# Graph attention kernel: first-tile scores straight from the parts of q and k, and softmax reciprocals turned by VectorE and spread by DMA

## The chip, the cores and the metric

The kernel runs on one core of one Trainium2 chip. The metric is device time in microseconds (us). Three runs of the kernel before took 1132.78, 1135.05 and 1135.31 us; the median is 1135.05 us.

## The reference

`x` is (8, 1024, 256), `adj` (1024, 1024) with zeros and ones, all fp32; there are 8 heads of 32 lanes.

```
h = relu(layernorm(x))
q, k, v = h @ Wq + bq, h @ Wk + bk, h @ Wv + bv          # split into 8 heads of 32
scores = einsum('bqhd,bkhd->bhqk', q, k) / sqrt(32) + (1 - adj) * -1e9
out = einsum('bhqk,bkhd->bqhd', softmax(scores), v)      # (b, n, 256)
x + out @ Wo + bo
```

## The kernel before

**Order of the work.** A batch is done in two phases of four heads (PHASES, g = 0 and 1). A phase has 32 rows; a row is one head h for one tile of 128 queries against all 1024 keys. Eight rows (two query tiles, four heads) are a unit; row r = 0 to 7 of it. Every engine walks over the same 8 x 2 x 32 = 512 rows in a function `slot`, and its order within a slot is written out by hand: tables with one entry per r (SCORES_AHEAD, MASK_AHEAD, EXP_AHEAD say how many rows ahead each step is; EXP_AT, HIGH_AT, COPY_AT, TAKE_AT say where in the slot it stands), STEPS (in which rows TensorE does the quarters, called pieces, of a projection) and ACT_COPIES (which rows' second copy ScalarE does; VectorE does the others). Engines are tied by semaphores alone.

**A row.** TensorE makes the scores (L703) from `q_stack` and `k_stack`. VectorE adds the mask and takes the row minimum (L550) into `rows`, a ring of four. ScalarE takes the exponential and the row's sum (L456). TensorE turns the row in eight 128x128 transposes (L717, `turn`) into the two banks `ps_turn`; ScalarE copies the first (L461), VectorE or ScalarE the second (L557, L466). `ps_scores` has two buffers, so that scores of row n wait for the mask of row n-2.

**The stacks.** q and k are each split into a high and a low float32r part (L471 on ScalarE, L562 on VectorE). Four parts of 32 lanes, stacked on the 128 partitions, make one full matmul give the exact product: (q_hi, q_lo, q_hi, q_lo) by (k_hi, k_hi, k_lo, k_lo). The parts go to the stacks by DMAs (L288, `stack_step`), 16 of 64 KB for 512 tokens. SP's queue issues them, at the start also GpSimd's and ScalarE's; SP also loads x, masks and residuals and stores the output.

**A unit's end.** In slot r = 7 VectorE takes the reciprocals of the sums (L585, `invert`), GpSimd spreads each over 32 columns (L425, `spread`), TensorE turns these in two transposes (L766, `turn_inv`), ScalarE copies them (L492, `copy_inv`). In slot 0 of the next unit TensorE multiplies the turned rows by v (64 matmuls, L780, `heads`) into `ps_heads`, and in slot 1 VectorE scales (L591, `norm_heads`). The output projection (L751) waits for that. `ps_heads` also takes the transposes of the next batch's normed x (L740), at HT_ROWS.

**The start.** TensorE projects q and k of all tokens (L724 in START_STEPS), then v (L733), then the row for the output bias (L812, added by L632), and then makes the scores of five rows, each after its stacks have landed, before the first `turn`. SP loads the masks of tiles 2 and 3 and stacks q's second half after the first four scores.

Of the kernel before, what the change touches and what calls it, by code (L numbers as in the profile page):

```python
# [10 lines left out]
P = 128  # L11
# [17 lines left out]


SCORES_AHEAD = (4, 5, 4, 4, 5, 4, 4, 5)
MASK_AHEAD = (4, 4, 4, 3, 3, 3, 3, 3)
EXP_AHEAD = (3, 2, 2, 2, 2, 2, 2, 1)
# [3 lines left out]
EXP_AT = (2, 2, 0, 0, 2, 2, 2, 0)  # L37
HIGH_AT = (0, 1, 1, 0, 0, 0, 1, 2)
COPY_AT = (0, 0, 0, 1, 1, 1, 1, 1)
TAKE_AT = (0, 1, 1, 0, 1, 0, 2, 2)  # L40
# [10 lines left out]
INV_ROW, NORM_ROW = 7, 1  # L51
# [3 lines left out]
def place(u, r):  # L55
# [28 lines left out]
STATS = (0, 1, 7, 7, 16, 23, 23, 23)  # L84

ACT_COPIES = (
    (2, 3, 4, 11, 13, 18, 21, 24, 27, 30),
    (0, 3, 6, 8, 10, 11, 13, 16, 19, 21, 24, 27, 29),
# [29 lines left out]
def gnn_kernel(nc, x, adj, Wq, bq, Wk, bk, Wv, bv, Wo, bo, out):  # L118
# [5 lines left out]
    with ExitStack() as ctx:  # L124
# [22 lines left out]
        start_parts = [nc.alloc_sbuf_tensor_at(f"start_{n}", [P, BANK], F32R, offset=turned_at + k * BANK * 4)  # L147
# [39 lines left out]
        ACT_HEADS = 2  # L187
# [107 lines left out]
        def _(sp):  # L295
# [76 lines left out]
        def _(pool):  # L372
# [44 lines left out]
            stack_step(pool, 0, 3, pool_stacked, range(ACT_HEADS, ACT_HEADS + 1))  # L417
# [17 lines left out]
            for b in range(BATCH):  # L435
                for g in range(PHASES):
                    for u in range(UNITS):
                        spread(b, g, u)
                        if (b, g, u) == (0, 0, 0):
                            late_masks(3, MASKS_LATE, TILES)  # L440
# [11 lines left out]
        def _(act):  # L452
# [52 lines left out]
            act.wait_ge(lo_done, START_QK.index(3) + 1)  # L505
            stack_step(act, 0, 3, start_stacked, range(ACT_HEADS))
            for n in range(EXP_AHEAD[-1]):
                exp(n)

            def slot(b, g, i, first, last):  # L510
                n, r = row(b, g, i), i % UNIT_ROWS
                pb, pg, kind, s = step_ended(b, g, i)
                if r == 0 and not (first and i == 0):
                    copy_inv(unit(b, g, i // UNIT_ROWS) - 1)
# [5 lines left out]
                if (g, i - 1) in HT_ROWS and not last:  # L520
                    copy_ht(b + 1, HT_ROWS[g, i - 1])
# [15 lines left out]
            copy_inv(BATCH * BATCH_UNITS - 1)  # L537

        @block.vector
        def _(dve):  # L540
# [39 lines left out]
            def invert(b, g, u, first):  # L580
                dve.wait_ge(exp_done, row(b, g, u * UNIT_ROWS) + UNIT_ROWS)
                if not (first and u == 0):

                    dve.wait_ge(inv_spread, unit(b, g, u))
                nc.vector.reciprocal(row_inv[:], row_sum[:, u % 2, :]).then_inc(inv_done, 1)  # L585

            def norm_heads(k, g, u):
                dve.wait_ge(inv_copied, k + 1)
                dve.wait_ge(heads_done, k + 1)
                dst = heads_t[0][:, u * UNIT_Q:(u + 1) * UNIT_Q] if g == 0 else heads_t[1][:, u % 2, :]  # L590
                nc.vector.tensor_tensor(dst, ps_heads[:, 0:UNIT_Q], inv_t, ALU.mult  # L591
# [17 lines left out]

            dve.sem_inc(copied_b, START)  # L610
# [10 lines left out]
            for k, s in enumerate(START_QK):  # L621
                low_part(k + 1, 0, s, (start_lo + lo)[s][:], (start_hi + hi)[s][:], QK_BANKS[k % 2])
                if k == 1:
                    dve.wait_ge(mask_in[1], 16)
                    nc.vector.tensor_scalar(mask[:, 1:MASKS_EARLY, :], mask[:, 1:MASKS_EARLY, :], 1.0, -MASKED,
                                            ALU.subtract, ALU.mult).then_inc(mask_start_ready, 1)
            for s in range(V_STEPS):
                copy_v(0, 0, s, V_BANKS[s])

            dve.wait_ge(weights_in, 4 * 16)  # L630
            dve.wait_ge(bo_done, 1)
            nc.vector.tensor_tensor(bo_row[:], BO_BANK, bo_row[:], ALU.add).then_inc(bo_ready, 1)  # L632
            for n in range(MASK_AHEAD[-1]):
                mask_row(n)
# [251 lines left out]
```

## Time and profile before

| | |
|---|---|
| median of three runs | 1135.05 us |
| profiled execution | 1133.49 us |
| its span in the trace | 1131.3 us |
| busy TensorE / ScalarE / VectorE / GpSimd | 1108.3 / 1018.6 / 960.8 / 154.4 us |
| share of TensorE's work on the chain that ended last | 90% |
| DMA | 99.52 MB, mean 88 GB/s |

PE is TensorE's matmul side, PEld its weight load, DVE VectorE, ACT ScalarE, POOL GpSimd, SP SyncE; a name with a q (SPq) is the issue of DMAs. Ends of matmuls are modelled, so PE at 100% is not PE at its peak; starts of groups are the safer reading. A releaser behind "<-" is what ended the idle time before an instruction. Shares of a whole run are means over stages; what bounds a stage is read from that stage.

### The profile page before, as it was taken

To read this page: it belongs to the slowest core of one execution; us is meant where nothing else is said; L and a number is where in the kernel's file an instruction comes from. 1 tells how busy PE (TensorE), PEld (TensorE's weight loads), DVE (VectorE), ACT (ScalarE), POOL (GpSimd) and SP (SyncE) were. 2 spreads that over 40 slices of the span, in tenths; PEclk is the share of its full clock that TensorE was granted. 3 is DMA by queue.
4 is the path that set the end of the run, shared out by engine and by line. 5 is a ranking of instruction groups with operands and counts; after the bars stand their busy time and mean duration, and the time that the engine had idled before them with its cause. 6 is when DMAs were issued, how large, how long until landed. Compare 5 with 4: busy or idle time off the path is not lost.

```text
span 1131.3 us, 28240 instructions
## 1 busy us (share of the span) xinstructions
PE 1108.3 (98%) x10776; PEld 904.2 (80%) x10776; DVE 960.8 (85%) x1747; ACT 1018.6 (90%) x1883; POOL 154.4 (14%) x248
## 2 busy tenths in 40 slices
PE   7899999999999999999999999999999999999997
PEld 6677887888878888888887888888887888878775
DVE  4698889988899888997889988998889988888875
ACT  2689999999999999999999999999999999999995
POOL 5342100021002100120001200002100021000001
PEclk9799999999999999999999999999999999999999
DMA  7651342324323243332424324242342324223101
GB/s 204 212 125 44 76 131 58 94 57 123 85 76 94 55 133 77 83 86 56 130 63 108 80 57 125 64 107 63 77 127 61 93 58 103 67 76 93 41 20 38
DMA packets 77860, 99.52 MB, mean 88 GB/s; under 512 B 18528, under 2 KB 44256, under 8 KB 77728
## 3 DMA queue, kind: packets, MB, share of 16 engines
q1 hardware_dynamic: 76704, 95.89, 32.3%
q8 instruction: 87, 1.43, 0.5%
q0 software_dynamic: 640, 1.31, 0.5%
q10 hardware_dynamic: 384, 0.52, 0.2%
q14 instruction: 45, 0.37, 0.1%
HBM read 22.15 MB, written 8.39 MB: 27 GB/s over the span
## 4 chain that ended last, share of the span: by engine, by line
PE 90%; ACT 5%; DVE 1%; DMA 1%; SPq 1%; issue 1%; ACTq 1%; DVEq 0%
PE ps_turn L717 29%; PE ps_scores L703 22%; PE ps_heads L780 18%; PE ps_side L724 9%; PE ps_side L733 5%; PE ps_side L751 5%; ACT rows L456 3%; ACT turned_a L461 1%; SPq L288 1%; PE ps_heads L740 1%; PE ps_heads L766 1%; PE ps_turn L724 1%; ACTq L288 0%; DMA xn<-in_x 0%; ACT turned_b L466 0%
## 5 line engine op out<-in xcount | busy, mean ns | idle before, releaser
L550 DVE CUSTOM_DVE_ANT_0 rows<-ps_scores,mask 128x1024 f32<-128x1024 f32 x512 | 612.7, 1214 | 27.8 <-PE ps_scores L703 24.1
L456 ACT ACTIVATE rows<-rows,row_min 128x1024 f32<-128x1024 f32 x512 | 587.2, 1151 | 12.7 <-DVE row_min L550 12.7
L717 PE MATMUL ps_turn<-ident_r,rows_raw 128*128 128x128 f32 x4096 | 463.5, 257 | 8.0 <-ACT turned_a L461 5.3
L717 PEld LDWEIGHTS ps_turn<-ident_r,rows_raw 128*128 128x128 f32 x4096 | 399.8, 141 | 75.8 <-issue 34.7
L461 ACT ACTIVATE turned_a<-ps_turn 128x512 f32<-128x512 f32 x512 | 305.7, 597 | 53.9 <-PE ps_turn L717 53.6
L703 PE MATMUL ps_scores<-k_stack,q_stack 128*128 128x512 f32 x1024 | 317.7, 422 | 6.0 <-DMA k_stack<-k_lo 5.4
L557 DVE COPY turned_b<-ps_turn 128x512 f32<-128x512 f32 x328 | 225.6, 688 | 37.7 <-PE ps_turn L717 30.8
L703 PEld LDWEIGHTS ps_scores<-k_stack,q_stack 128*128 128x128 f32 x1024 | 168.2, 190 | 27.7 <-issue 7.8
L425 POOL COPY inv_wide<-row_inv 128x256 f32<-128x256 f32 x64 | 25.5, 399 | 906.2 <-DVE row_inv L585 906.2
L780 PE MATMUL ps_heads<-turned_a,v 128*32 128x256 f32 x2048 | 123.8, 382 | 0.6 <-ACT inv_wide L492 0.6
L780 PE MATMUL ps_heads<-turned_b,v 128*32 128x256 f32 x2048 | 122.4, 379 | 0.0
L466 ACT ACTIVATE turned_b<-ps_turn 128x512 f32<-128x512 f32 x184 | 109.3, 594 | 0.0
L780 PEld LDWEIGHTS ps_heads<-turned_b,v 128*32 128x32 f32 x2048 | 68.3, 110 | 42.2
L456 ACT ACTIVATION_READ_ACCUMULATOR rows<-rows,row_min 128x1 f32 x512 | 100.7, 197 | 0.0
L780 PEld LDWEIGHTS ps_heads<-turned_a,v 128*32 128x32 f32 x2048 | 61.5, 109 | 37.0 <-ACT turned_a L461 0.7
L591 DVE TENSOR_TENSOR heads_t<-ps_heads,inv_wide 128x256 f32<-128x256 f32 x64 | 27.1, 424 | 55.1 <-PE ps_heads L780 55.1
L733 PE MATMUL ps_side<-wv,ht 128*128 128x128 f32 x496 | 69.7, 281 | 0.0
L751 PE MATMUL ps_side<-wo,heads_t 128*128 128x256 f32 x256 | 68.1, 389 | 0.7 <-DVE heads_t L591 0.7
L724 PE MATMUL ps_side<-ht,wq 128*128 128x256 f32 x240 | 64.5, 391 | 0.0
L733 PEld LDWEIGHTS ps_side<-wv,ht 128*128 128x128 f32 x496 | 62.5, 191 | 2.1
L724 PE MATMUL ps_side<-ht,wk 128*128 128x256 f32 x240 | 63.7, 388 | 0.0
L751 PEld LDWEIGHTS ps_side<-wo,heads_t 128*128 128x128 f32 x256 | 46.0, 190 | 7.0 <-issue 1.2
(68 smaller groups left out, 595.4 us busy)
## 6 DMA issues: line engine op xcount, KB each, us to landing
q_stack<-q_hi SPq DMA_DIRECT2D x248, 64.0 KB, 2.0
q_stack<-q_lo SPq DMA_DIRECT2D x248, 64.0 KB, 2.0
k_stack<-k_hi SPq DMA_DIRECT2D x242, 64.0 KB, 2.0
k_stack<-k_lo SPq DMA_DIRECT2D x242, 64.0 KB, 2.0
res<-in_x SPq DMA_DIRECT2D x32, 256.0 KB, 2.8
out<-res SPq DMA_DIRECT2D x32, 256.0 KB, 2.5
xn<-in_x SPq DMA_DIRECT2D x7, 1024.0 KB, 5.9
mask<-in_adj SPq DMA_DIRECT2D x1, 2048.0 KB, 8.3
```

The costliest lines, as they stand in the source:

```text
L456: nc.scalar.activation(rows[:, k, :], rows[:, k, :], ACT.Exp, bias=row_min[:, k:k + 1], scale=-1.0, accum_out=row_sum[:, u % 2, j:j + 1]). ...
L461: nc.scalar.activation(turned[0][:, place(i // UNIT_ROWS, i % UNIT_ROWS)], ps_turn[0][:], ACT.Copy).then_inc(copied_a, 1)
L466: nc.scalar.activation(turned[1][:, place(i // UNIT_ROWS, i % UNIT_ROWS)], ps_turn[1][:], ACT.Copy).then_inc(copied_b, 1)
L550: nc.vector.tensor_tensor_reduce(out=rows[:, k, :], in0=ps_scores[n % 2][:], in1=mask[:, qt, :], scale=1.0, scalar=START_MIN, op0=ALU.add, ...
L557: nc.vector.tensor_copy(turned[1][:, place(i // UNIT_ROWS, i % UNIT_ROWS)], ps_turn[1][:]).then_inc(copied_b, 1)
L591: nc.vector.tensor_tensor(dst, ps_heads[:, 0:UNIT_Q], inv_t, ALU.mult).then_inc(heads_normed, 1)
L703: mm = nc.tensor.matmul(ps_scores[n % 2][:, c * BANK:(c + 1) * BANK], q_stack[g][:, h, qt * P:(qt + 1) * P], k_stack[g][:, h, c * BANK:(c ...
L717: tr = nc.tensor.transpose(ps_turn[half][:, k, :].bitcast(F32R), rows_raw[:, n % RING, kt * P:(kt + 1) * P], ident_r[:])
L724: mm = nc.tensor.matmul(bank[:, cols], w[n][:, k, g * P:(g + 1) * P], ht[:, k, s // 2 * BANK:(s // 2 + 1) * BANK][:, cols], start=(k == 0) ...
L733: mm = nc.tensor.matmul(bank[:, t * P:(t + 1) * P], ht[:, k, tok], w["v"][:, k, g * P:(g + 1) * P], start=(k == 0), stop=(k == DCH - 1))
L751: mm = nc.tensor.matmul(ps_side[:, t * DIM:(t + 1) * DIM], lhs, w["o"][:, g, :], start=(g == 0), stop=(g == PHASES - 1))
L780: mm = nc.tensor.matmul(ps_heads[h * HEAD_DIM:(h + 1) * HEAD_DIM, 0:UNIT_Q] .rearrange("p (t n) -> p t n", n=P), v[g][:, half * PARTS + kt ...
```

## The change

**Start.** Rows 0 to 3 (the first query tile, four heads) no longer use the stacks. Their scores are made from the 32-lane parts as they stand in SBUF: four terms (hi hi, lo hi, hi lo, lo lo) for each 512 keys, accumulated in PSUM, two rows interleaved. That is 16 matmuls with a contraction of 32 for two rows. Rows 0 and 1 come right after the third q/k step, rows 2 and 3 after the fourth, the bias row ahead of them; v is projected after them. The fifth row's scores move behind the first `turn`. The start's last stacks are issued in another division: ScalarE 1 head, GpSimd 2, SP 1 (before 2, 1, 1).

**Reciprocals.** `spread`, `turn_inv` and `copy_inv` go. VectorE takes the reciprocals in slot 6, waits for them, and turns them in 32x32 squares. GpSimd writes the result to a DRAM buffer in one DMA (128 pieces of 128 bytes), waits for it, and reads it back in four DMAs, one for each head, each spread to 32 partitions (2 x 512 bytes on each). VectorE scales at the end of slot 2, after these four have landed.

**Tables.** Rows ahead, places in the slot, the pieces' rows (STEPS), HT_ROWS and ACT_COPIES (23 of 64 rows before, 25 after) are written anew, and the late masks are made in two parts.

```diff
-SCORES_AHEAD = (4, 5, 4, 4, 5, 4, 4, 5)
-MASK_AHEAD = (4, 4, 4, 3, 3, 3, 3, 3)
-EXP_AHEAD = (3, 2, 2, 2, 2, 2, 2, 1)
-EXP_AT = (2, 2, 0, 0, 2, 2, 2, 0)
-INV_ROW, NORM_ROW = 7, 1
+SCORES_AHEAD = (4, 4, 4, 4, 5, 4, 4, 5)
+MASK_AHEAD = (4, 4, 3, 3, 3, 3, 3, 3)
+EXP_AHEAD = (1, 3, 2, 2, 2, 2, 2, 1)
+EXP_AT = (0, 0, 0, 0, 0, 0, 2, 0)
+INV_ROW, NORM_ROW = 6, 2
...
-    (("qk", 0, (2, 2, 3, 3)), ("qk", 1, (5, 5, 5, 6)), ("o", 2, (10, 10, 11, 11)), ("qk", 2, (13, 13, 14, 14)),
-     ("v", 0, (18, 18, 19, 19)), ("qk", 3, (21, 21, 22, 22)), ("o", 3, (26, 26, 27, 27)), ("v", 1, (29, 29, 30, 31))),
+    (("qk", 0, (2, 2, 3, 3)), ("qk", 1, (5, 5, 6, 6)), ("o", 2, (9, 10, 11, 11)), ("qk", 2, (13, 13, 14, 14)),
+     ("v", 0, (17, 18, 19, 19)), ("qk", 3, (21, 21, 22, 22)), ("v", 1, (25, 26, 27, 27)), ("o", 3, (28, 29, 29, 30))),
+    (("qk", 0, (1, 2, 3, 3)), ("qk", 1, (5, 5, 5, 6)), ("v", 0, (9, 10, 11, 11)), ("qk", 2, (13, 13, 14, 14)),
+     ("o", 0, (17, 18, 19, 19)), ("qk", 3, (21, 21, 22, 22)), ("o", 1, (25, 26, 27, 27)), ("v", 1, (29, 29, 30, 30))),
...
-HT_ROWS = {(0, 28): 0, (0, 30): 1, (1, 1): 2, (1, 4): 3}
+HT_ROWS = {(0, 29): 0, (0, 30): 1, (1, 4): 2, (1, 6): 3}
-START_STEPS = (("ht", 0), ("ht", 1), ("qk", 0), ("qk", 1), ("ht", 2), ("ht", 3), ("qk", 3), ("qk", 2),
-               ("v", 0), ("v", 1))
+START_STEPS = (("ht", 0), ("ht", 1), ("qk", 0), ("qk", 1), ("ht", 2), ("ht", 3), ("qk", 3), ("bo", 0), ("rows", 0),
+               ("qk", 2), ("rows", 2), ("v", 0), ("v", 1))
...
-            def spread(b, g, u):
-                pool.wait_ge(inv_done, unit(b, g, u) + 1)
-                pool.wait_ge(inv_turned, unit(b, g, u) + START)
-                pool.tensor_copy(inv_wide[:], row_inv[:].unsqueeze(2).to_broadcast([P, UNIT_ROWS, HEAD_DIM])
-                                 ).then_inc(inv_spread, 1)
+            def turn_inv(b, g, u):
+                by_head = inv_rows[0:UNIT_ROWS].rearrange("(t h) q -> h t q", h=PARTS)
+                k = unit(b, g, u)
+                pool.wait_ge(inv_squares, k + 1)
+                if k:
+                    pool.wait_ge(inv_in, k * PARTS * 16)
+                pool.dma_start(inv_rows.rearrange("j (c q) -> c j q", q=SQUARE), inv_turned[:]).then_inc(inv_out, 16)
+                pool.wait_ge(inv_out, (k + 1) * 16)
+                if k:
+                    pool.wait_ge(heads_normed, k)
+                for h in range(PARTS):
+                    pool.dma_start(inv_t[h * HEAD_DIM:(h + 1) * HEAD_DIM, :, :],
+                                   by_head[h].partition_broadcast(HEAD_DIM)
+                                   ).then_inc(inv_in, 16)
...
-            def copy_inv(k):
-                act.wait_ge(inv_turned, k + 1 + START)
-                nc.scalar.activation(inv_t, ps_heads[:, UNIT_Q:], ACT.Copy).then_inc(inv_copied, 1)
...
-                nc.vector.reciprocal(row_inv[:], row_sum[:, u % 2, :]).then_inc(inv_done, 1)
+                nc.vector.reciprocal(row_inv[:, 0:UNIT_ROWS], row_sum[:, u % 2, :]).then_inc(inv_done, 1)
+                dve.wait_ge(inv_done, unit(b, g, u) + 1)
+                nc.vector.transpose(inv_turned[:], row_inv[:]).then_inc(inv_squares, 1)
...
             def norm_heads(k, g, u):
-                dve.wait_ge(inv_copied, k + 1)
+                dve.wait_ge(inv_in, (k + 1) * PARTS * 16)
                 dve.wait_ge(heads_done, k + 1)
...
+            def start_scores(first):
+                pe.wait_ge(lo_done, START_QK.index(3) + 1)
+                if first == 0:
+                    pe.wait_ge(bo_ready, 1)
+                else:
+                    pe.wait_ge(masked, first)
+                for c in range(CHUNKS):
+                    k_hi, k_lo = ((start_hi[1], start_lo[1]), (hi[1], lo[1]))[c]
+                    terms = ((start_hi[0], k_hi), (start_lo[0], k_hi), (start_hi[0], k_lo), (start_lo[0], k_lo))
+                    for j, (q_part, k_part) in enumerate(terms):
+                        for n in (first, first + 1):
+                            lanes = slice(n * HEAD_DIM, (n + 1) * HEAD_DIM)
+                            mm = nc.tensor.matmul(ps_scores[n % 2][:, c * BANK:(c + 1) * BANK], q_part[lanes, 0:P],
+                                                  k_part[lanes, :], start=(j == 0), stop=(j == PARTS - 1))
...
-            def turn_inv(b, g, u, first, last):
...
-                for t in range(UNIT_TILES):
-                    tr = nc.tensor.transpose(ps_heads[:, UNIT_Q + t * P:UNIT_Q + (t + 1) * P].bitcast(F32R),
-                                             inv_wide_raw[:, t * PARTS:(t + 1) * PARTS].rearrange("p h d -> p (h d)"),
-                                             ident_r[:])
-                tr.then_inc(inv_turned, 1)
```

## Rows read from the trace of the kernel before

**Rows 1.** Busy time in one steady batch, by engine, beside the granted clock.
```profile
core 0: us, PE busy (x) PEld busy (x) DVE busy (x) ACT busy (x) POOL busy (x), PEclk, DMA share, GB/s
396.70:532.40 135.70, 135.70 (x1345) 111.55 (x1345) 119.40 (x218) 126.88 (x236) 15.51 (x27) 1.00 0.33 87
```

**Rows 2.** Waits in that batch: who waited for whom, total, times, longest.
```profile
DVE heads_t L591 <- PE ps_heads L780: 5.8, 6, 1.5
...
PEld ps_scores L703 <- DVE row_min L550: 0.4, 2, 0.3
```

**Rows 3.** Timeline of TensorE in one unit: start, length, group.
```profile
406.26 1.16 PE L703 MATMUL ps_scores<-k_stack,q_stack 128*128 128x512 f32 x4
...
407.89 1.10 PE L724 MATMUL ps_side<-ht,wq 128*128 128x256 f32 x4
...
411.50 1.17 PE L703 MATMUL ps_scores<-k_stack,q_stack 128*128 128x512 f32 x4
412.50 0.29 PE L766 MATMUL ps_heads<-ident_r,inv_wide_raw 128*128 128x128 f32 x2
...
413.40 1.93 PE L780 MATMUL ps_heads<-turned_a,v 128*32 128x256 f32 x32
```

**Rows 4.** Groups of instructions in the whole run: busy, mean ns, idle before.
```profile
L492 ACT ACTIVATE inv_wide<-ps_heads 128x256 f32<-128x256 f32 x64 | 24.8, 387 | 14.2 <-PE ps_heads L766 13.0
...
L766 PE MATMUL ps_heads<-ident_r,inv_wide_raw 128*128 128x128 f32 x128 | 18.5, 226 | 0.0
...
L585 DVE RECIPROCAL row_inv<-row_sum 128x8 f32<-128x8 f32 x64 | 12.4, 194 | 0.0
```

**Rows 5.** Chain of work that ended last: start and length of three units' products.
```profile
446.99 3.59 PE ps_heads L780 x64
...
463.93 3.59 PE ps_heads L780 x64
...
480.62 3.59 PE ps_heads L780 x64
```

**Rows 6.** DMA issues: count, KB each, median us from issue to landing.
```profile
out<-res SPq DMA_DIRECT2D x32, 256.0 KB, 2.5
xn<-in_x SPq DMA_DIRECT2D x7, 1024.0 KB, 5.9
...
q_stack<-start_q_hi POOLq DMA_DIRECT2D x8, 64.0 KB, 2.8
...
k_stack<-k_lo POOLq DMA_DIRECT2D x2, 64.0 KB, 4.2
```

**Rows 7.** Timeline of VectorE, slot 6 of a unit and slot 2 of the next.
```profile
408.44 1.22 DVE L550 CUSTOM_DVE_ANT_0 rows<-ps_scores,mask 128x1024 f32<-128x1024 f32 x1
...
419.65 0.69 DVE L557 COPY turned_b<-ps_turn 128x512 f32<-128x512 f32 x1
```

**Rows 8.** Timeline of the start, all engines, in order of time.
```profile
19.38 0.50 POOL L288 DMA_DIRECT2D q_stack<-start_q_hi  x1
...
20.30 0.75 DVE L562 SCALAR_TENSOR_TENSOR k_lo<-ps_turn,bk_col,k_hi 128x512 fp32r<-128x512 f32 x1 [2.47 <-ACT k_hi L471]
...
21.05 1.95 PE L733 MATMUL ps_side<-wv,ht 128*128 128x128 f32 x16
...
25.75 0.42 DVE L632 TENSOR_TENSOR bo_row<-ps_scores,bo_row 128x256 f32<-128x256 f32 x1 [0.24 <-PE ps_scores L812]
...
29.64 0.70 PE L703 MATMUL ps_scores<-k_stack,q_stack 128*128 128x512 f32 x2 [4.00 <-DMA k_stack<-k_lo]
...
35.63 0.39 SPq L318 DMA_DIRECT2D mask<-in_adj  x1
36.06 0.22 PEld L717 LDWEIGHTS ps_turn<-ident_r,rows_raw 128*128 128x128 f32 x1
...
47.67 0.69 ACT L471 ACTIVATE q_hi<-ps_side,bq_col 128x512 fp32r<-128x512 f32 x1 [1.57 <-DMA q_stack<-q_lo]
```

**Rows 9.** Busy time and granted clock around the first rows, columns as in 1.
```profile
30.00:40.00 10.00, 6.67 (x26) 4.41 (x25) 5.92 (x10) 4.06 (x8) 0.00 (x0) 0.54 0.45 134
```

**Rows 10.** Timeline of the last units: TensorE's products, the last reciprocals and scaling.
```profile
1090.71 1.93 PE L780 MATMUL ps_heads<-turned_a,v 128*32 128x256 f32 x32
...
1106.85 1.93 PE L780 MATMUL ps_heads<-turned_a,v 128*32 128x256 f32 x32
...
1119.62 0.19 DVE L585 RECIPROCAL row_inv<-row_sum 128x8 f32<-128x8 f32 x1
...
1125.48 0.42 DVE L591 TENSOR_TENSOR heads_t<-ps_heads,inv_wide 128x256 f32<-128x256 f32 x1 [3.20 <-PE ps_heads L780]
```

More of the change, by code:

```diff
@@ L437, in _ @@
                     for u in range(UNITS):
-                        spread(b, g, u)
-                        if (b, g, u) == (0, 0, 0):
-                            late_masks(3, MASKS_LATE, TILES)
+                        turn_inv(b, g, u)
+                        if (b, g) == (0, 0) and u < 2:
+                            late_masks(3, MASKS_LATE + 2 * u, MASKS_LATE + 2 * u + 2)
                         if g == 0 and u < 2 and b > 0:
@@ L504, in _ @@
                     high_part(k + 1, 0, s, (start_hi + hi)[s][:], QK_BANKS[k % 2])
[L505 to L508, printed above, removed]
+                elif (kind, s) == ("rows", 0):
+                    act.wait_ge(lo_done, START_QK.index(3) + 1)
+                    stack_step(act, 0, 3, start_stacked, range(ACT_HEADS))
+                    for n in range(EXP_AHEAD[-1]):
+                        exp(n)
             def slot(b, g, i, first, last):
@@ L519, in slot @@
                         exp(m)
-                if (g, i - 1) in HT_ROWS and not last:
-                    copy_ht(b + 1, HT_ROWS[g, i - 1])
+                row_before = (g, i - 1) if i else (0, ROWS - 1)
+                if row_before in HT_ROWS and not last and (g or i):
+                    copy_ht(b + 1, HT_ROWS[row_before])
                 if kind == "qk" and HIGH_AT[r] == 1:
@@ L626, in _ @@
                                             ALU.subtract, ALU.mult).then_inc(mask_start_ready, 1)
+                elif k == 2:
+                    dve.wait_ge(weights_in, 4 * 16)
+                    dve.wait_ge(bo_done, 1)
+                    nc.vector.tensor_tensor(bo_row[:], BO_BANK, bo_row[:], ALU.add).then_inc(bo_ready, 1)
+                    for n in range(2):
+                        mask_row(n)
+            for n in range(2, MASK_AHEAD[-1]):
+                mask_row(n)
             for s in range(V_STEPS):
                 copy_v(0, 0, s, V_BANKS[s])
[L630 to L634, printed above, removed]
             def slot(b, g, i, first, last):
@@ L638, in slot @@
                 ended = step_ended(b, g, i)
-                if r == NORM_ROW and not (first and u == 0):
-                    norm_heads(unit(b, g, u) - 1, *((g, u - 1) if u else (1 - g, UNITS - 1)))
                 if r == INV_ROW:
@@ L654, in slot @@
                     take(*ended)
+                if r == NORM_ROW and not (first and u == 0):
+                    norm_heads(unit(b, g, u) - 1, *((g, u - 1) if u else (1 - g, UNITS - 1)))
                 for t in range(TILES):
@@ L754, in project_out @@
                     mm.then_inc(o_done, 1)
[L756 to L769 removed]
             def heads(k, parity, g, half):
                 pe.wait_ge((copied_a, copied_b)[half], (k + 1) * UNIT_ROWS + START)
[L774 to L776 removed]
+                if half == 0 and k:
+                    pe.wait_ge(heads_normed, k)
+                    b, gu = k // BATCH_UNITS, (k // UNITS % PHASES, k % UNITS)
+                    if gu in HT_UNITS and b < BATCH - 1:
+                        pe.wait_ge(ht_done, (b + 1) * HT_STEPS + HT_UNITS[gu])
                 for kt in range(PARTS):
@@ L793, in _ @@
             for kind, s in START_STEPS:
-                for piece in range(PIECES):
-                    if kind == "ht":
+                if kind == "ht":
+                    for piece in range(PIECES):
                         if s % DCH == 0:
@@ L798, in _ @@
                         turn_ht(s, piece, HT_BANKS[s % 2])
[L799 to L814 removed]
+                elif kind == "qk":
+                    k = START_QK.index(s)
+                    pe.wait_ge(weights_ready, 1)
+                    pe.wait_ge(ht_done, (s // DCH + 1) * DCH)
+                    if k >= 2:
+                        pe.wait_ge(lo_done, k - 1)
+                    for piece in range(PIECES):
+                        qk(0, s, piece, QK_BANKS[k % 2])
+                elif kind == "v":
+                    for piece in range(PIECES):
+                        values(0, s, piece, V_BANKS[s])
+                elif kind == "rows":
+                    start_scores(s)
+                else:
+                    pe.wait_ge(weights_in, 4 * 16)
+                    for g in range(PHASES):
+                        mm = nc.tensor.matmul(BO_BANK, bias["v"][:, g:g + 1].to_broadcast([P, P]), w["o"][:, g, :],
+                                              start=(g == 0), stop=(g == PHASES - 1))
+                    mm.then_inc(bo_done, 1)
             pe.wait_ge(lo_done, QK_STEPS)
[L817 to L819 removed]
             def slot(b, g, i, first, last):
@@ L824, in slot @@
                 turn(b, g, i, 1)
+                if row(b, g, i) == 0:
+                    for m in range(PARTS, SCORES_AHEAD[-1]):
+                        scores(m)
                 for m in reach(SCORES_AHEAD, row(b, g, i)):
@@ L829, in slot @@
                         heads(unit(b, g, u) - 1, u + 1, g if u else 1 - g, half)
-                if r == INV_ROW:
-                    turn_inv(b, g, u, first, last)
                 if (g, i) in HT_ROWS and not last:
```

79 lines of the change are left out of this document (29 added, 50 removed), and 2 rows, old and new, of the table STEPS.

## The prediction, made before the changed kernel ran

> **What bounds the kernel now.** I read the busy time of one steady batch first, because the whole run mixes a start, a steady part and an end. In a batch of 135.70 us TensorE has no idle time, ScalarE is busy 126.88 us and VectorE 119.40 us, at the full granted clock of 1.00 (2.4 GHz) [rows 1]. The waits of the same batch say the same: TensorE waits 0.4 us for VectorE's masks, and VectorE waits 5.8 us for TensorE's products before it scales them [rows 2]. So between the start and the last phase the order of TensorE's instructions sets the time; ScalarE has 8.8 us of room in a batch, VectorE 16.3. Next I read the timeline of a unit, to price groups by the distance of their starts, since ends of matmuls are modelled. Last I read the start, where TensorE waits, and the last units.
>
> **Two transposes and their copy go (steady part).** From the scores at 406.26 to the side group at 407.89 there are scores and a turn: 1.63 us. From the scores at 411.50 to the products at 413.40 there are scores, two transposes of reciprocals and a turn: 1.90 us [rows 3]. The two transposes cost 0.27 us of issue, not the 0.45 us that twice their modelled 226 ns would give [rows 4]. Eight in a batch are 8 x 0.27 = 2.2 us, and as TensorE is the bound the batch is shorter by that. ScalarE loses 8 x 387 ns = 3.1 us in a batch [rows 4] and gets two more second copies, about 0.6 us each, 1.2 us: it ends at 125.0 us of about 134, no nearer to being the bound. VectorE loses two copies (0.69 us each [rows 7], 1.4 us) and gets eight 32x32 turns with a wait for the reciprocals before each. No row shows such a turn; a reciprocal takes 194 ns [rows 4], a copy of 512 columns 0.69 us [rows 7]; with 32 columns it is next to the first, and I take 0.2 us, and 0.1 us for the wait, 2.4 us in all. At the upper end it would be 6.3 us. Either fits into its 16.3 us, so both cost nothing as long as that room stands between the same events.
>
> **New order of TensorE's groups.** Counted in the tables, side pieces of a batch form 33 groups before and 40 after, and scores 5 groups in a unit before and 6 after: 7 + 8 = 15 more changes of work in a batch. The price: the unit from 446.99 to 463.93 (16.94 us) has one step of two split as 3 and 1 pieces, the next one to 480.62 (16.69 us) two steps of the same matmuls split as 2 and 2 [rows 5]. A worse split thus costs up to 0.25 us, part of it a late mask. For a plain extra group I take 0.06 us (bounds 0 and 0.12), 15 x 0.06 = 0.9 us; phase 0's step split 3 and 1 becomes 2 and 2 and gives 0.25 us back. Net cost 0.65 us in a batch, bounds -0.25 and 1.55. The move of HT_ROWS to neighbouring rows 29 and 30 makes TensorE wait for one ScalarE copy that stands first in its slot; I count that within these bounds. Steady gain: 2.2 - 0.65 = 1.5 us in a batch, bounds 0.6 and 2.4. It holds for 7.5 batches (the last phase is bound otherwise): 11.3 us, bounds 4.5 and 18.
>
> **The reciprocals' way through DRAM.** This is the added wait. VectorE waits at the end of slot 2 for four DMAs; behind it on VectorE stand the masks and second copies of slot 3, and TensorE's turns and scores wait for these. The time at hand runs from the start of slot 6 (408.44) to the end of the copy in the next unit's slot 2 (419.65 + 0.69 = 420.34): 11.9 us [rows 7]. The time needed: reciprocal and turn 0.4, hand-over 0.2, first DMA's landing, three more issues by GpSimd at 0.5 us [rows 8], last landing. No row shows a 16 KB write in pieces of 128 bytes; the nearest are GpSimd's DMAs at the start, 2.8 us in the middle and 4.2 us where all queues were full, and the store to DRAM, 2.5 us [rows 6]. In the steady part the DMA engines are 33% busy [rows 1], so I take 2.8 for each: 0.6 + 2.8 + 1.5 + 2.8 = 7.7 us, with 4.2 for each 10.5 us. Both are under 11.9, so the wait is hidden and costs nothing; beyond about 12 us every microsecond is VectorE's, less the 2.0 us that it is idle in a unit (16.3 / 8). GpSimd has nothing else that is late: it is busy 15.5 us of a batch [rows 1]. A wait for exponentials does not come in either: the tables put the exponential of row 7 first in ScalarE's slot 5.
>
> The store of 256 KB lands after 2.5 us and the load of 1 MB after 5.9 us [rows 6], so most of a small transfer is fixed time. The Trainium skill, page "DMA: Bandwidth & Descriptors", section "Anatomy of one DMA — SWDGE (gpsimd) path", gives 2.0 us plus size by 436 GB/s for a DMA issued by GpSimd, by which two in a row and the issues would be an estimated 6.2 us; but it warns that the completion of a write to HBM can be surprisingly long. That second rule speaks against this change; it is the slower rival below, and no row here shows a small write.
>
> **The start.** Before, TensorE's first scores wait 4.00 us for a stack and begin at 29.64; five rows of scores come before the first turn, whose weights load at 36.06 [rows 8]. After: k's low part ends at 20.30 + 0.75 = 21.05, the bias row takes VectorE 0.42 more, so rows 0 and 1 begin at 21.5. Their 16 matmuls of 512 columns cost 0.25 us each (four in 1.00, from 411.50 to 412.50 [rows 3]), 4.0 us if they run one after another. The two rows use different lanes of the array. The products, which use four different column strips, show what such sharing gives: 64 matmuls of 256 columns in 3.59 us [rows 5], 0.056 each. I take 2.2 us for two rows (bounds 2.0 and 4.0). Then q's second half 1.9 us to 25.6 (as v's, nearly the same work), meanwhile two masks of 1.22 us to 26.2, rows 2 and 3 to 28.4, v's two steps 1.95 us each [rows 8] to 32.3: first turn 3.8 us earlier. With matmuls one after another this is 21.5 + 4.0 + 1.9 + 0.7 (masks) + 4.0 + 3.9 = 36.0, no gain. What is late next: SP loads the mask at 35.63, after the fourth row's scores; afterwards it is held only by its own queue, which frees at about 31.9, 3.7 us earlier, so the stack for which ScalarE waits until 47.67 [rows 8] lands by as much earlier. ScalarE also runs further ahead with its exponentials, and TensorE, which no longer stands still for 4 us, should not fall to the lower clock (mean 0.54 in the stretch from 30 to 40 us, that is mostly 1.2 GHz [rows 9]); I keep the sum of these at 0.2 us, since the stacks pace that stretch. Gain 4.0 us, bounds 0 and 7.
>
> There is a rule for such narrow matmuls: the Trainium skill, page "TensorE: Matmul & The Clock Gate", section "Measured speedup vs the span model", states 3.07 times the speed for four row strips. It would put two rows near my value; no row of this trace shows row strips.
>
> **The end.** In the last phase ScalarE sets the pace, as there are no q, k and v steps: a unit takes 1106.85 - 1090.71 = 16.14 us [rows 10]. Without its copy it takes 0.39 us less [rows 4], 1.5 us for four units. The last unit's wait for that copy, 0.5 us, goes too. But there no other work hides the DMAs: from the last reciprocals at 1119.62 to the scaling at 1125.48 there are 5.9 us [rows 10], and with the reciprocals a slot (about 2.0 us) earlier 7.9, against 7.7 needed. I take a cost of 0.5 us, bounds 0 and 4.
>
> **Sum.** 11.3 + 4.0 + 1.5 + 0.5 - 0.5 = 16.8 us. The profiled execution took 1133.49 us (span 1131.3), so 1116.7 after. The median of the runs before stands 1.56 us above it; 1118.3, rounded 1118. The bounds of the terms give gains from about 3 to 28 us, 1107 to 1132, hardly all at one end.
>
> **Rivals.**
> First, the new order eats the gain. ScalarE's 125 of 134 us and TensorE's changes of work leave little room, and each slot's order is new. For it: the split of 3 and 1 already cost 0.25 us through a late mask. If each of the 15 extra groups costs 0.12 and the neighbouring transposes of x another 0.5 us, a batch gains 2.2 - 1.8 + 0.25 - 0.5 = 0.15 us, 1 us in all; with start and end (5.5 us) that gives about 1128, and a microsecond a batch of new waits more would give 1136. Against it: TensorE waits only 0.4 us in a batch now. Chance 0.17, of which 0.07 faster by over 0.3%, 0.08 within, 0.02 slower.
>
> Second, slower: the way through DRAM is longer than the time at hand. It decides above 11.9 + 2.0 = 13.9 us. If the write in 128-byte pieces and each spread read land in 6 us (the 5.9 of a megabyte load [rows 6]), the way is 0.6 + 6 + 1.5 + 6 = 14.1 us, and no gain is lost yet; at 15 us VectorE is 1.1 us late in each of 64 units, 70 us, which would give about 1188. With GpSimd issues of 1 us and a write of 8 us it is near this. Against it: 4.2 us was the worst median with all queues full. Chance 0.12.
>
> Third, the change does not do what it says at the start: the narrow matmuls run one after another. Then 1122. Chance 0.16, inside the forecast's sign and range.
>
> **Chances.** Forecast 0.55 (1108 to 1126), the third 0.16, the first 0.17, the second 0.12. About 0.3% (3.4 us) is what a measurement can tell from no change. Faster: 0.55 + 0.16 + 0.07 = 0.78; within: 0.08; slower: 0.02 + 0.12 = 0.14. The range from 1107 to 1131 leaves out the slower rival and some of the first one's upper end.
>
> **What would show it.** The steps are right if a steady batch is about 134.2 us with TensorE without idle time and no L766; if VectorE's scaling waits for no DMA; if scores begin at 21.5 and the first turn at about 32; if the granted clock from 30 to 40 us is near 1.00; and if the last scaling waits under 1 us. A steady batch over 135.5 us with waits of TensorE for rows or masks speaks for the first rival, a DMA as releaser of the scaling for the second. The prediction is wrong as a whole if a batch is paced by another engine.

## The result, and the profile after

The changed kernel took 1128.16 us in the median (kernel before in the same runs: 1134.12 us); ratio 0.9947, 95% interval 0.9936 to 0.9958. It is faster by 6.0 us, 0.53%, clear of noise, and well short of the 16.8 us forecast. One of its 17 executions took 2503.03 us and is left out of the ratio; the other 16 lie between 1123.86 and 1133.14 us.

Steady batches first. The windows are cut from the start of one batch's first products (L810, `heads`) to the next one's; columns as in [rows 1].

```profile
core 0: us, PE busy (x) PEld busy (x) DVE busy (x) ACT busy (x) POOL busy (x), PEclk, DMA share, GB/s
189.85:325.59 135.74, 135.03 (x1329) 109.59 (x1328) 119.12 (x224) 124.48 (x230) 35.00 (x59) 1.00 0.38 96
869.48:1003.83 134.35, 134.35 (x1330) 109.75 (x1329) 118.62 (x222) 124.09 (x230) 34.88 (x59) 1.00 0.35 88
```

One batch lasts 135.74 us, as long as the 135.70 of [rows 1], another 134.35. In the first TensorE has 0.7 us of idle time; before it had none in any of the six full batches. The waits between 190 and 1004 us (columns as in [rows 2]) name it:

```profile
DVE heads_t L609 <- DMA inv_t<-inv_rows: 7.0, 5, 2.1
...
PEld ps_turn L759 <- DVE turned_b L572: 3.7, 5, 1.4
```

Five times VectorE's scaling waits for a DMA, and five times TensorE then waits for VectorE's copy. One such place in time order:

```profile
269.84 0.20 DVE L601 RECIPROCAL row_inv<-row_sum 128x8 f32<-128x8 f32 x1
270.07 0.21 DVE L603 STREAM_TRANSPOSE inv_turned<-row_inv 128x32 f32<-128x32 f32 x1
...
270.58 0.71 POOL L438 DMA_DIRECT2D inv_rows<-inv_turned  x1 [9.86 <-DVE inv_turned L603]
...
273.44 2.11 POOL L444 DMA_DIRECT2D inv_t<-inv_rows  x4 [2.15 <-DMA inv_rows<-inv_turned]
273.55 0.58 SPq L305 DMA_DIRECT2D xn<-in_x  x1
...
282.08 0.42 DVE L609 TENSOR_TENSOR heads_t<-ps_heads,inv_t 128x256 f32<-128x256 f32 x1 [1.45 <-DMA inv_t<-inv_rows]
...
284.30 0.54 PE L759 MATMUL ps_turn<-ident_r,rows_raw 128*128 128x128 f32 x4 [0.65 <-DVE turned_b L572]
```

The four reads are issued at 273.44, SP's load of 1 MB of x at 273.55, and the last read lands at 282.08, 6.5 us after the end of the reads' issue (275.55). The way took 12.2 us; VectorE was ready after 10.8 (282.08 - 1.45 - 269.84). The same load stood at nearly the same place in the kernel before, 1.3 us ahead of the same products (0.7 us after the change), but no one waited for a small DMA behind it:

```profile
276.35 0.58 SPq L297 DMA_DIRECT2D xn<-in_x  x1
```

In the changed kernel the wait appears in five of the six batches that load x at this place. In the first one the load is issued at 137.85, 0.9 us ahead of the reads at 138.73, the scaling waits for nothing, and the unit takes 16.51 us.

The start, to be read against [rows 8]:

```profile
20.98 0.75 DVE L577 SCALAR_TENSOR_TENSOR k_lo<-ps_turn,bk_col,k_hi 128x512 fp32r<-128x512 f32 x1 [2.47 <-ACT k_hi L491]
...
22.20 0.50 PE L745 MATMUL ps_scores<-start_k_hi,start_q_hi 32*128 32x512 f32 x2 [1.18 <-DVE bo_row L651]
...
24.27 3.63 PE L766 MATMUL ps_turn<-ht,wq 128*128 128x256 f32 x8
...
33.46 0.78 PEld L759 LDWEIGHTS ps_turn<-ident_r,rows_raw 128*128 128x128 f32 x8
...
37.41 0.54 PE L759 MATMUL ps_turn<-ident_r,rows_raw 128*128 128x128 f32 x4 [2.08 <-DVE turned_b L572]
```

The first turn is at 33.46 instead of 36.06, in an execution whose k low part began 0.68 us later (20.98 against 20.30), so 3.3 us earlier. But the second row's turn waits 2.08 us for a copy that stands behind two masks on VectorE. That part begins at 20.3 to 23.8 us in the profiled executions of all the kernels here, so places in the start are compared by their distance from it.

### The profile page after: what moved, and what is told of

Read it like the earlier page. It is cut to its first block, busy times and chain, and to the rows that moved or that the text cites. A ratio compares the mean times of both kernels' runs of the same rounds, so it can differ in the third digit from the quotient of the medians.

```text
span 1127.8 us, 28288 instructions
## 1 busy us (share of the span) xinstructions
PE 1103.4 (98%) x10672; PEld 890.5 (79%) x10672; DVE 958.4 (85%) x1796; ACT 998.9 (89%) x1835; POOL 314.4 (28%) x508
## 4 chain that ended last, share of the span: by engine, by line
PE 37%; issue 29%; DMA 19%; POOL 10%; DVE 1%; ACT 1%; SPq 0%; POOLq 0%; DVEq 0%; ACTq 0%
PE ps_turn L759 11%; DMA inv_t<-inv_rows 9%; DMA inv_rows<-inv_turned 9%; PE ps_scores L726 9%; PE ps_heads L810 8%; POOL inv_t L444 6%; PE ps_side L766 3%; PE ps_side L793 2%; POOL xn L412 2%; PE ps_side L775 2%; POOL mask L451 2%; POOL ln_t L397 1%; DVE rows L565 1%; DMA mask<-in_adj 1%; ACT rows L476 1%
## 5 line engine op out<-in xcount | busy, mean ns | idle before, releaser
L476 ACT ACTIVATE rows<-rows,row_min 128x1024 f32<-128x1024 f32 x512 | 589.7, 1159 | 10.9 <-DVE row_min L565 10.8
L759 PE MATMUL ps_turn<-ident_r,rows_raw 128*128 128x128 f32 x4096 | 468.3, 258 | 13.3 <-DVE turned_b L572 7.9
L726 PE MATMUL ps_scores<-k_stack,q_stack 128*128 128x512 f32 x1016 | 330.6, 424 | 0.5 <-DVE row_min L565 0.2
L572 DVE COPY turned_b<-ps_turn 128x512 f32<-128x512 f32 x312 | 214.9, 689 | 87.1 <-PE ps_turn L759 82.0
L438 POOL DMA_DIRECT2D inv_rows<-inv_turned x64 | 46.4, 725 | 635.5 <-DVE inv_turned L603 630.1
L444 POOL DMA_DIRECT2D inv_t<-inv_rows x256 | 135.5, 536 | 144.0 <-DMA inv_rows<-inv_turned 139.7
L726 PEld LDWEIGHTS ps_scores<-k_stack,q_stack 128*128 128x128 f32 x1016 | 159.3, 188 | 18.2 <-DVE row_min L565 8.8
L810 PE MATMUL ps_heads<-turned_a,v 128*32 128x256 f32 x2048 | 123.8, 382 | 0.4 <-ACT turned_a L481 0.4
L810 PE MATMUL ps_heads<-turned_b,v 128*32 128x256 f32 x2048 | 122.2, 379 | 0.0
L486 ACT ACTIVATE turned_b<-ps_turn 128x512 f32<-128x512 f32 x200 | 120.0, 600 | 0.4 <-PE ps_turn L759 0.4
L476 ACT ACTIVATION_READ_ACCUMULATOR rows<-rows,row_min 128x1 f32 x512 | 105.8, 207 | 0.0
L810 PEld LDWEIGHTS ps_heads<-turned_b,v 128*32 128x32 f32 x2048 | 66.6, 110 | 43.9
L810 PEld LDWEIGHTS ps_heads<-turned_a,v 128*32 128x32 f32 x2048 | 60.0, 109 | 38.0 <-ACT turned_a L481 0.5
L793 PE MATMUL ps_side<-wo,heads_t 128*128 128x256 f32 x256 | 72.6, 389 | 0.7 <-DVE heads_t L609 0.7
L775 PEld LDWEIGHTS ps_side<-wv,ht 128*128 128x128 f32 x496 | 67.6, 191 | 7.1 <-issue 0.4
```

The costliest lines, as they stand in the source:

```text
L444: pool.dma_start(inv_t[h * HEAD_DIM:(h + 1) * HEAD_DIM, :, :], by_head[h].partition_broadcast(HEAD_DIM)).then_inc(inv_in, 16)
L476: nc.scalar.activation(rows[:, k, :], rows[:, k, :], ACT.Exp, bias=row_min[:, k:k + 1], scale=-1.0, accum_out=row_sum[:, u % 2, j:j + 1]). ...
L486: nc.scalar.activation(turned[1][:, place(i // UNIT_ROWS, i % UNIT_ROWS)], ps_turn[1][:], ACT.Copy).then_inc(copied_b, 1)
L572: nc.vector.tensor_copy(turned[1][:, place(i // UNIT_ROWS, i % UNIT_ROWS)], ps_turn[1][:]).then_inc(copied_b, 1)
L726: mm = nc.tensor.matmul(ps_scores[n % 2][:, c * BANK:(c + 1) * BANK], q_stack[g][:, h, qt * P:(qt + 1) * P], k_stack[g][:, h, c * BANK:(c ...
L759: tr = nc.tensor.transpose(ps_turn[half][:, k, :].bitcast(F32R), rows_raw[:, n % RING, kt * P:(kt + 1) * P], ident_r[:])
```

## The experiments

All are compared with the kernel before, run beside them. A difference "by the ratio" is the ratio's, taken of 1134 us; where it and the difference of the medians disagree, both are given. "Batch" is the distance between the starts of the products of two batches' first units, read from the timelines, for the six full batches after the first.

| kernel | ratio to before, interval | batch, us |
|---|---|---|
| before | 1 | 135.65 to 135.76 |
| changed | 0.9947, 0.9936 to 0.9958 | 134.35 to 137.74 |
| later scaling | 0.9925, 0.9906 to 0.9944 | 134.80 to 135.43 |
| earlier x load | 0.9911, 0.9892 to 0.9929 | 134.34 to 134.52 |
| both | 0.9909, 0.9892 to 0.9926 | 134.79 to 135.04 |
| changed, no way through DRAM | 0.9871, 0.9849 to 0.9892 | 134.36 to 134.53 |
| before, no transposes, no copy | 0.9912, 0.9897 to 0.9927 | 134.34 to 134.45 |
| before, no copy | 0.9995, 0.9983 to 1.0007 | 135.67 to 135.68 |
| before, new start | 0.9972, 0.9960 to 0.9984 | 135.69 to 135.77 |
| before, new start, no transposes | 0.9871, 0.9855 to 0.9888 | 134.34 to 134.72 |
| before, new tables | 1.0156, 1.0142 to 1.0170 | 138.13 to 138.20 |
| earlier x load, later scaling at the ends | 0.9896, 0.9875 to 0.9917 | 134.36 to 134.52 |

### Is it the wait for the reads, and does the x load make it?

Theory: the reads collide with the 1 MB load once a batch. Rival: the new tables eat the gain. Second rival: the small transfers are late by themselves. A unit is measured here from the start of its products to the start of the next unit's; unit (1,1) is the one whose scaling waits.

```diff
-INV_ROW, NORM_ROW = 6, 2
+INV_ROW, NORM_ROW = 6, 3
```

> The changed kernel with the scaling of a unit one slot later (end of slot 3 instead of slot 2, about 1.6 us more room). Theory: the way of the reciprocals through DRAM is late once a batch, when the 1 MB load of x for a later batch is issued at the same moment as the four reads; in the changed kernel's trace this makes the unit (1,1) last 17.3 to 19.8 us instead of 16.55, 6.9 us in seven batches, and about 2 us in the first unit. Then this kernel takes 6 to 8 us less than the changed one, about 1120 to 1122, and that unit is back at about 16.6 us. Rival: the late reads only use up room that VectorE has anyway, and the missing gain lies in the new order of groups; then the time stays at 1126 to 1129.

Measured 1124.82 us, 3.3 us less than the changed kernel (2.5 by the ratio), short of the 6 to 8 expected. The unit meant is at 16.6 us in five of seven batches, 17.05 and 16.73 in two. So the wait made that unit long, but this cure costs something: units with transposes of x (L782) take 17.41 and 17.53 us instead of 17.29 and 17.42, so a batch stays near 135.0.

```diff
-                            if g == 1 and s == 1 and b + 2 < BATCH:
+                            if g == 1 and s == 0 and b + 2 < BATCH:
                                 sp.wait_ge(ht_turned, (b + 2) * HT_STEPS)
                                 load_x(b + 2)
```

> The changed kernel with the 1 MB load of x issued one stacking step earlier in SP's queue, some 10 us before the reads of the reciprocals, nothing else. Theory (the load is what makes the reads late): unit (1,1) is back at 16.6 us, 5 to 7 us less than the changed kernel, 1121 to 1123. Rival (the small transfers are late by themselves, by the stacks' traffic or by GpSimd's issue): unit (1,1) stays at 17.3 us or more, time 1126 to 1129.

Measured 1123.18 us, 5.0 us less than the changed kernel (4.1 by the ratio, 1.6 to 6.6). The same unit in this run:

```profile
262.57 0.58 SPq L305 DMA_DIRECT2D xn<-in_x  x1
...
273.76 2.11 POOL L444 DMA_DIRECT2D inv_t<-inv_rows  x4 [2.05 <-DMA inv_rows<-inv_turned]
...
280.96 0.42 DVE L609 TENSOR_TENSOR heads_t<-ps_heads,inv_t 128x256 f32<-128x256 f32 x1
```

The load goes 11 us ahead of the reads; the scaling has no releaser in brackets, it waited for nothing. The unit takes 16.51 to 16.54 us in every batch. That decides for the load: the small transfers, the stacks' traffic and GpSimd's issues are the same as in the changed kernel. One of the five collisions has a second party. In the batch where the unit takes 19.77 us GpSimd stands idle before the last read:

```profile
679.89 1.59 POOL L444 DMA_DIRECT2D inv_t<-inv_rows  x3 [2.00 <-DMA inv_rows<-inv_turned]
680.38 0.59 SPq L305 DMA_DIRECT2D xn<-in_x  x1
683.53 0.53 POOL L444 DMA_DIRECT2D inv_t<-inv_rows  x1 [2.06 <-issue]
```

With the earlier load the same pause stands before the same read (at 680.91) and the scaling waits for nothing. So load and pause together made this unit, the load alone the other four.

> Later scaling (slot 3) and earlier x load together. Theory: both remove the same collision, so it is no better than the better of them by more than 1 us: 1119 to 1122, faster than the changed kernel and than the one before. Rival (two separate costs): it gains the sum of the two, below 1118.

Measured 1123.43 us, no better than the earlier load alone, though above the 1119 to 1122 expected: the two cures remove one cost, not two, and the later scaling still costs 0.45 us a batch.

Without the way (the diff in its core):

```diff
-                        turn_inv(b, g, u)
...
-                    dve.wait_ge(inv_out, unit(b, g, u) * 16)
...
-                dve.wait_ge(inv_in, (k + 1) * PARTS * 16)
+                dve.wait_ge(inv_zeroed, 2)
...
+            nc.vector.memset(inv_t[:], 1.0).then_inc(inv_zeroed, 1)
```

> The changed kernel without the way through DRAM: GpSimd issues none of the five DMAs, the scaling multiplies by a constant tile of ones and waits for the products alone, so the output is not normalised. Theory: all of what the way costs, waits and traffic, is 7 to 9 us: 1119 to 1121, steady batches of 134.3 us. Rival (the new order of groups eats the gain): the time is within 2 us of the changed kernel's, 1126 to 1128, and batches of 135.3 us remain.

Measured 1119.54 us, 8.6 us less than the changed kernel. So the way through DRAM costs 8.6 us in all (5.9 to 11.3 by the two ratios' intervals). 4 to 5 of it are the x load's collisions; the traffic itself is nearly free in steady batches, 134.5 us with it (earlier x load) and without.

### What TensorE's two transposes were worth

```diff
-                if r == INV_ROW:
-                    turn_inv(b, g, u, first, last)
+                if r == INV_ROW and (g, u) in HT_UNITS and not last:
+                    pe.wait_ge(ht_done, (b + 1) * HT_STEPS + HT_UNITS[g, u])
...
-                if r == 0 and not (first and i == 0):
-                    copy_inv(unit(b, g, i // UNIT_ROWS) - 1)
```

> The kernel before without the two transposes of the reciprocals on TensorE and without ScalarE's copy of them: VectorE scales with the unturned tile, so the output is wrong by the order of the reciprocals; reciprocals and GpSimd's spreading stay, the tables stay. Step of the prediction: 0.27 us a unit, 2.2 us a batch, that is 16 to 18 us less, about 1117. Rival (the price read from start to start is too high; the changed kernel's units fell from 16.75 to 16.58 us only): 0.17 us a unit, 11 us less, about 1123.

Measured 1123.85 us, 10 us less (8.3 to 11.7): the rival's value. A batch falls by 1.3 us, 0.16 us a unit. The timeline of TensorE shows where 0.27 came from:

```profile
410.35 1.16 PE L699 MATMUL ps_scores<-k_stack,q_stack 128*128 128x512 f32 x4
411.35 0.80 PE L713 MATMUL ps_turn<-ident_r,rows_raw 128*128 128x128 f32 x8
412.08 1.93 PE L777 MATMUL ps_heads<-turned_a,v 128*32 128x256 f32 x32
```

Scores and a turn ahead of products take 1.73 us (412.08 - 410.35); ahead of a side group they take 1.63 [rows 3]. The prediction subtracted the second from 1.90; the right difference is 1.90 - 1.73 = 0.17.

The copy alone is left out by dropping `copy_inv` and its waits and letting the scaling wait for the transposes:

> The kernel before with TensorE's two transposes of the reciprocals in place and ScalarE's copy of them left out (the scaling multiplies by the unturned tile, so the output is wrong by the order of the reciprocals). If TensorE's issue alone is the price in the steady part, batches stay near 135.7 us and only the last phase gains, 1 to 2 us in all, 1132. Rival: ScalarE's copy carries the price (8.8 us of room in a batch are not room at the place of the copy); then most of the 9.9 us of e5 show here, 1124 to 1127.

Ratio 0.9995, batch 135.67: TensorE's issue is the price, ScalarE's 0.39 us a unit were free under the old tables. In the last phase, where the prediction had ScalarE set the pace, the units take 15.78, 18.02 and 16.16 us without the copy, 15.73, 17.98 and 16.14 with it. Only the last unit gets shorter, 14.84 to 14.45.

### The start, and whether the parts add up

The new START_STEPS, `start_scores`, the order of masks and copies on VectorE and the stacks' division, all else as before:

> The kernel before with the new start alone (first-tile scores from the parts, order of the start, division of the stacks), all tables and the reciprocals' way as before. Step of the prediction: 4.0 us less, 1130, first products of TensorE about 4 us earlier than 55.41. Rival (the start's gain is given back in the second unit, as in the changed kernel's trace, where 3.3 us at the first products are 2.5 us one batch later): 2 us less or less than that, 1132 or more.

Measured 1130.98 us, ratio 0.9972: 2.7 us by the medians, 3.2 by the ratio. The first products come 31.88 us after k's low part instead of 35.11, 3.2 us earlier. The forecast's 4.0 was somewhat too high, the rival's 2 too low; both lie within the interval's 1.8 to 4.5, so the place in the trace decides.

> The kernel before with the new start and without the reciprocals' transposes and copy (e5 and e6 together, old tables; output wrong by the order of the reciprocals). If start and transposes add up: 9.9 + 2.7 us less, 1121, and the new tables with their scaling in slot 2 are worth at most 2 us beside them (1119.5 without the way). Rival: the new tables cost what the prediction put on them, 5 us; then this kernel is at 1115.

Measured 1118.49 us, ratio 0.9871. The median lies midway between the theory's 1121 and the rival's 1115. By ratios, 0.88% and 0.28% add to 1.16%, measured 1.29%: they add up within the intervals, and the rival's 19 us lie outside (12.5 to 16.4). The changed kernel without its way has the same ratio, so the new tables cost 0 there, give or take 3 us, against the 4.9 us of the prediction. The batches say it more sharply: 134.51 us for most with the new tables, 134.34 to 134.45 with the old ones and no transposes, but for one of 134.72. That is about 0.1 us a batch, where 0.65 were forecast.

### The new tables in the old kernel

SCORES_AHEAD to TAKE_AT, STEPS, HT_ROWS, STATS and ACT_COPIES from the changed kernel, reciprocals as before:

> The kernel before with the changed kernel's tables alone (rows ahead, places in the slot, rows of the pieces, HT_ROWS, ScalarE's copies, statistics), the reciprocals in slot 7 and scaling in slot 1 as before. Step of the prediction: the 15 more changes of work cost 0.65 us a batch net, about 5 us more, 1139. Rival: they cost nothing (same, 1134), and the missing gain lies in the DMAs alone. Second rival: 1 us a unit group or more through new waits, 1145.

Measured 1151.71 us, 17.7 us more, beyond all three expectations: 2.5 us a batch. One place where it arises, turns of row 1, first in this kernel and then in the changed one:

```profile
404.72 0.88 PE L717 MATMUL ps_turn<-ident_r,rows_raw 128*128 128x128 f32 x8
...
405.83 0.58 ACT L461 ACTIVATE turned_a<-ps_turn 128x512 f32<-128x512 f32 x1
...
406.56 0.34 PE L717 MATMUL ps_turn<-ident_r,rows_raw 128*128 128x128 f32 x2
```

```profile
667.86 0.88 PE L759 MATMUL ps_turn<-ident_r,rows_raw 128*128 128x128 f32 x8
...
668.46 0.61 ACT L481 ACTIVATE turned_a<-ps_turn 128x512 f32<-128x512 f32 x1
...
669.48 0.88 PE L759 MATMUL ps_turn<-ident_r,rows_raw 128*128 128x128 f32 x8
```

With `copy_inv` still ahead of three exponentials, ScalarE copies 1.11 us after the turn's start instead of 0.60, and the next turn comes 1.84 us after it instead of 1.62. This place gives 0.22 us of the 0.31 that a unit loses; the rest was not followed. It suggests that the copy that was free under the old tables is not free under the new ones. That is not shown: this kernel also keeps the two transposes and scales in slot 1 instead of 2, and no run takes the copy alone from it.

### What remains at the ends

```diff
-                if r == NORM_ROW and not (first and u == 0):
+                if r == NORM_ROW + ((first and u == 1) or (last and g == 1)) and not (first and u == 0):
```

This goes together with the earlier x load.

> The changed kernel with the x load one stacking step earlier, and the scaling one slot later only where the other runs showed it late: the first unit and the last phase. Theory: e2 (1123.2) keeps the steady batch of 134.5 us; its first unit (20.98 us against 17.68 in e3) and its last unit (15.78 against 14.44) give 2.3 and 1.3 us back: 1119 to 1121, about the time without any way through DRAM (1119.5). Rival: these waits are only moved to the next slot, or the 3.7 us are traffic and not waits; then it stays at 1122 to 1124.

Measured 1120.76 us, ratio 0.9896: this beats both kernels, by 13.6 us the one before (11.8 by the ratio), and lies within the expected 1119 to 1121. From the kernel with the earlier x load alone (0.9911) the intervals do not tell it apart; the units do. Its second unit takes 18.08 us instead of 20.98. Its last one takes 15.71 us, no better than 15.78: the theory was right on the first and wrong on the last.

The second unit first. In the changed kernel the first write is issued at 47.91, behind a 2 MB mask load (43.08) and a 1 MB x load (43.70), and lands 6.1 us after it, against 2.5 in the median. GpSimd waits 5.61 us for it instead of about 2:

```profile
54.28 2.16 POOL L444 DMA_DIRECT2D inv_t<-inv_rows  x4 [5.61 <-DMA inv_rows<-inv_turned]
...
61.02 0.42 DVE L609 TENSOR_TENSOR heads_t<-ps_heads,inv_t 128x256 f32<-128x256 f32 x1 [1.90 <-DMA inv_t<-inv_rows]
...
63.24 0.53 PE L759 MATMUL ps_turn<-ident_r,rows_raw 128*128 128x128 f32 x4 [1.70 <-DVE turned_b L572]
```

The last unit is not a DMA's work. A group of four side matmuls, 1.10 us elsewhere, takes 1.94 there, and the window around it shows the clock:

```profile
1112.95 1.94 PE L793 MATMUL ps_side<-wo,heads_t 128*128 128x256 f32 x4
```

```profile
1112.50:1116.50 4.00, 4.00 (x22) 3.42 (x21) 0.42 (x2) 2.82 (x6) 0.71 (x1) 0.57 0.06 4
```

The granted clock is 0.57 in these 4 us, that is mostly 1.2 GHz instead of 2.4. In the kernel without the way the same stretch is at 1.00 and the unit takes 14.37 us. TensorE's waits just ahead are alike, 0.62 and 0.76 us in the changed kernel, 0.63 and 0.77 without the way. Of the five kernels with the way the clock falls there in three (last unit 15.71 to 15.80 us) and not in the two that scale later throughout (14.43 and 14.44). Why one run falls there and another does not was not settled; the kernel before also has a unit of 17.98 us in its last phase with a stretch at 0.57, where the kernel with the new start alone has 16.56.

## Why the prediction was wrong

By terms, in microseconds saved:

| step | forecast | measured |
|---|---|---|
| transposes and copy (steady, last phase, last wait) | 16.2 + 1.5 + 0.5 = 18.2 | 10.0 |
| new order of groups | -4.9 | 0 (two kernels of ratio 0.9871 each; about -0.7 by the batches) |
| start | 4.0 | 2.7 to 3.2 |
| way through DRAM | -0.5 | -8.6 |
| sum | 16.8 | 6.0 measured as a whole; the terms give 4.1 to 4.6 |

The measured terms come from runs of their own, each known to 1 to 3 us, so they need not add up better than this.

**The step that failed is the way through DRAM**, costed at nothing in steady batches and 0.5 us at the end; it took 8.6. The transposes were off by as much, but the new order took 4 to 5 us of that back; the last full batch, which loads no x, saves 1.3 us (135.65 to 134.35) where 1.5 were forecast. So the steady batch came out nearly right by luck, two errors of opposite sign, and the missing 10.8 us are mostly the way. Its normal length was right: 7.7 us forecast; at 269.84 the write is done after 3.6 us, and three issues and a median landing make 3.6 + 1.6 + 2.3 = 7.5. Wrong was the bound of 4.2 us for a landing "with all queues full" and the use of a mean DMA share of 33%. The 1 MB load and its 5.9 us stood in [rows 6] and were even used for the slower rival, but as a price for any landing, not as an event with a place in SP's queue. Its place could be read in the trace of before, at the end of unit (1, 1) (276.35, shown above). The time at hand was too long as well: 11.9 us by the old slots, 10.8 in the new ones. So the slower rival's mechanism was right, and its condition (15 us in every unit) wrong: it strikes at most once a batch. The first rival's time, 1128 us, is the one measured, but that is luck too: it had the new order eat the steady gain, and the new order ate about 0.1 us a batch.

**Transposes.** In steady batches the mechanism was right (TensorE's issue bounds, shown by the copy's 0.9995), the size 60% too high (0.27 against 0.16 to 0.17 us a unit), since two stretches were compared that end in different groups. In the last phase the mechanism was wrong: the copy was to give 1.5 us there and gave none; only the last unit's 0.4 us of the 0.5 are seen.

**New order.** The opposite error, about half as large: 0.06 us an extra group and a worse split were charged, and about 0.1 us a batch was lost in the changed kernel. A table's price depends on what else stands in the slot: the same tables cost 17.7 us beside the old transposes, copy and place of the scaling. These two errors hid each other in part: without the way the prediction's sum is 17.3, measured 14.6.

**Start.** The narrow matmuls do run in pairs: 16 from 22.20 to 24.27, 2.1 us (2.2 forecast). The third rival is out. Half of the serial 4.0 would be 2.0 us. The Trainium skill (page "TensorE: Matmul & The Clock Gate", section "Measured speedup vs the span model") has 3.07 times the speed for four row strips; this trace agrees in kind, about 1.9 times for two. What was missed is the clock:

```profile
24.00:28.00 4.00, 4.00 (x14) 2.69 (x12) 2.38 (x4) 1.24 (x2) 4.00 (x9) 0.57 1.02 294
```

TensorE had 1.2 us of idle time before 22.20, then 16 narrow matmuls, and is granted 0.57 from 24 to 28 us; q's second half takes 3.63 us instead of 1.89. The second 16 narrow matmuls run at 1.00 from 28 us. Between 30 and 40 us the clock is 0.89, where near 1.00 was expected and 0.54 stood before. The lower clock did not vanish; it became shorter and came earlier. Why it fell at 24 us was not tried.

**The end.** The last scaling waits 2.83 us for the products and not for the DMAs; this term was 0 instead of 0.5. In the profiled executions the last unit's lower clock makes 1.4 us of the difference between the changed kernel and the one without the way (15.80 against 14.37); whether that belongs to the way is open.

The second rule cited, that a write to HBM can complete surprisingly late (Trainium skill, page "DMA: Bandwidth & Descriptors", section "Anatomy of one DMA — SWDGE (gpsimd) path"), is not what decided: the small write lands in 2.5 us in the median, the reads in 2.3, and the long waits seen for them (in the changed kernel 6.1 us for the write, up to 7.0 for a read) stand beside megabyte loads.

## What to carry to other kernels

Cost a new DMA that someone waits for against the largest transfer that can be in flight at its place, by the issue times in the queue's timeline, not against a mean share. Read the price of a removed group from stretches that begin and end with the same kinds of groups. Before tuning tables around a late transfer, try to move the other transfer: one changed condition in SP's order gave back 4 to 5 of 8.6 us.

## What the runs showed of the hardware

**A stall of TensorE costs more than its length.** In the worst unit of the changed kernel the scaling waits 2.09 us and TensorE then 1.29 us, and the unit takes 19.77 instead of 16.55 us, 3.2 us more. Behind the wait the granted clock is 0.72:

```profile
689.28 0.42 DVE L609 TENSOR_TENSOR heads_t<-ps_heads,inv_t 128x256 f32<-128x256 f32 x1 [2.09 <-DMA inv_t<-inv_rows]
...
691.51 0.54 PE L759 MATMUL ps_turn<-ident_r,rows_raw 128*128 128x128 f32 x4 [1.29 <-DVE turned_b L572]
...
694.17 2.04 PE L766 MATMUL ps_side<-ht,wk 128*128 128x256 f32 x4
```

```profile
692.00:698.00 6.00, 5.94 (x30) 4.77 (x30) 4.80 (x11) 4.25 (x10) 0.71 (x1) 0.72 0.37 92
```

By estimate 6 us at 0.72 instead of 1.00 are worth 1.7 us, which with the 1.29 us of waiting makes 3.0 of the 3.2. After the shorter stall at 284.30 (0.65 us) the clock stays at 1.00 and the unit loses 1.2 us. These are two places of one execution.

**GpSimd's DMA issue.** A read to 32 partitions takes 533 ns of GpSimd in the median, the write in 128 pieces 717. Between them GpSimd stands idle once for 5.2 to 5.4 us and twice for 2.1 us with no releaser in the trace, in all five kernels here that have the way. In the changed kernel:

```profile
POOL inv_rows L438 <- issue: 5.4, 1, 5.4
...
POOL inv_t L444 <- issue: 4.1, 2, 2.1
```

One of the latter lies inside the 19.77 us unit. What causes them was not tried.
